# A three-layer sequence kernel on one core: slot outputs split over ScalarE and VectorE, the combine in fours, and the attention opening without its setup waits

## The chip, the cores and the metric

One core of one Trainium2 chip. The metric is the device time of one launch in microseconds (us), the median of several runs. Lower is better.

## What is computed

The reference, with names shortened, is a chain of four blocks over 4096 tokens of 256 features, each added to its input and followed by a layer norm. The inputs are float32.

```
x = _layernorm(x + conv_mlp(x))         # gated convolution block, then a two-layer MLP, 4 x 1024 tokens
x = _layernorm(x + experts(x))          # 32 experts, top 6 of a token, only 48 tokens per expert are served
x = _layernorm(x + attention(x))        # per branch of 1024 tokens: 16 heads of 16, rotary embedding
x = _layernorm(x + sparse_ffn(x))       # silu(gate) * up, 2 of each 4 kept, down

# in experts:
pos = jnp.take_along_axis(jnp.cumsum(oh, axis=0) - 1, flat_e[:, None], axis=1)[:, 0]
valid = pos < C                          # C = 48
slot = jnp.where(valid, flat_e * C + pos, E * C)
...
out = jnp.einsum('tk,tkh->th', topk_w.astype(x.dtype), y_pairs)
```

An expert serves the first 48 tokens that choose it, in token order. A token behind the point where all experts are full gets nothing from them. The chip's work on the expert outputs therefore touches only the first tiles of 128 tokens.

## The kernel before

The tokens are 32 tiles of 128 (`NT`), held in `x_sb` as [128, 32, 256]. Three functions follow one another: `conv_mlp_phase`, `experts_phase` and `attention_ffn_phase`. Each is a block in which every engine has its own program; the programs meet at semaphores only, and at a barrier between two blocks.

**End of the experts.** `experts_phase` computes 32 x 48 = 1536 slots. The experts' outputs lie transposed in `yT` (in the memory called arena). Twelve steps `j` (`CJ`) turn them: TensorE makes two 128x128 transposes into a PSUM bank `tp[j % 2]` (line 1038), VectorE multiplies them by the slots' weights into the high part `y[0]` (line 933, written in the matmul's float32r type), and VectorE again forms the low part `y[1]`, the product minus its high part (line 935). TensorE may fill the bank of step j once `y_ok` says that step j-2 is through with it. ScalarE's last instruction of the phase is the copy of the last expert's output (line 772).

**The combine.** A second block adds the slot outputs to the tokens. The generator `busy_pairs` (lines 1047 to 1056) is a loop over four groups of eight tiles with a branch on whether the group is reached by any slot, and in it a loop over four pairs of tiles with the same branch. In a pair, VectorE builds two one-hot matrices `hot[0]`, `hot[1]` of [128, 12, 128] (line 1068), TensorE sums 12 steps of high and low part for each tile into a bank of its own (line 1084, 24 matmuls per tile), and VectorE adds each bank to its tile (line 1074). A pair's one-hots wait until the pair before is summed (`cb_mm`), and its matmuls until the pair before is added (`cb_ok`). TensorE and VectorE load the branch's value from SBUF each for itself.

**Opening of the attention stage.** In `attention_ffn_phase` SyncE first starts the loads `mask`, `cos`, `sin`, `w_qk`, `w_v` (semaphore `consts`) and then four of the later weights. VectorE normalises the first branch's eight tiles in two halves (statistics at lines 1489 and 1495, the scaling at line 1504), with GpSimd computing the inverse deviation between (lines 1307 and 1310). GpSimd then fills constant columns of `v` and `qks` (lines 1323 to 1326; `setup` reaches 3 after them). VectorE casts the identity (line 1674) and writes eight constant columns (line 1678, `ready`). Both TensorE and ScalarE wait for `setup` 3 and `ready` 1 at their start:

```
            pe.wait_ge(consts, 16 * 5)
            pe.wait_ge(setup, 3)
            pe.wait_ge(ready, 1)
```

Then comes a loop over the eight tiles of the branch. TensorE transposes the tokens of a tile (line 1766, `x_transposed`, which waits for its half's layer norm through `ln_ok`), ScalarE copies them (line 1341), TensorE makes q, k and v (lines 1775 and 1777), ScalarE copies these (lines 1349 and 1352), VectorE rotates q and k (`rotate`, lines 1517 to 1524), ScalarE writes the high parts (line 1359 and two copies) and VectorE the low parts (`low_parts`, lines 1530 and 1531). VectorE's program has `rotate(0, t)` and `low_parts(0, t)` of one tile after another, so the rotation of the next tile follows the low parts of this one. When all eight are there, TensorE transposes q and k (`first_rows`, line 1782), finds the row maxima and starts the heads.

## Time and profile before

| | |
|---|---|
| median of 3 runs | 1910.19 us (1908.25 to 1912.74) |
| the profiled execution | 1904.56 us |
| its span, first to last instruction | 1902.7 us |
| mean granted clock of TensorE in it | 0.922 |
| busy: TensorE matmul / VectorE / ScalarE / GpSimd | 86% / 60% / 42% / 12% of the span |

The span is of one execution, and 1.9 us of its time lie around it. Times in the trace count from the start of the span. Busy shares are of the whole span, and a pipelined engine that is busy need not be at its best rate. PEclk is the share of TensorE's full clock of 2.4 GHz that the chip granted: 1.00 is 2.4 GHz, 0.50 is 1.2 GHz. What an engine waited for is inferred from the semaphores.

### The profile page before, as it was taken

How to read it: one execution, taken by the hardware profiler on the slowest of the kernel's cores; microseconds unless marked ns; L12 is line 12 of the kernel's file. 1: busy time of each engine (PE TensorE's matmuls, PEld its weight loads, DVE VectorE, ACT ScalarE, POOL GpSimd, SP SyncE). 2: the span in 40 equal slices, each digit the busy share in tenths (PEclk: the TensorE clock that was granted, in tenths of full speed). 3: DMA queues.
4: the chain of work that ended last, by engine and by line, in shares of the span. 5: the costliest groups of instructions: out<-in, count | busy, mean ns of one | idle time of the engine just before them, and what ended most of it. 6: DMA issues, size and time to landing. Idle time of an engine off the chain costs nothing.

```text
span 1902.7 us, 26419 instructions
## 1 busy us (share of the span) xinstructions
PE 1636.9 (86%) x10042; PEld 1007.7 (53%) x10043; DVE 1141.5 (60%) x2367; ACT 792.5 (42%) x1296; POOL 235.7 (12%) x237
## 2 busy tenths in 40 slices
PE   3899999986999964788899989899989899889797
PEld 3788888874558853333355433355433455433345
DVE  5556665647421144668558677568667578677465
ACT  5444444421212200437744157643167552177530
POOL 4333333311420001000000000100000100000100
PEclk8999999987999976759999989899989899988999
DMA  2000000005115502000000000000000000000000
GB/s 102 12 23 23 22 22 22 22 12 177 26 33 151 149 12 91 1 1 2 1 1 1 0 1 2 23 1 1 1 1 2 23 1 1 0 1 1 23 1 22
DMA packets 27147, 47.96 MB, mean 25 GB/s; under 512 B 7312, under 2 KB 16016, under 8 KB 26256
## 3 DMA queue, kind: packets, MB, share of 16 engines
q1 hardware_dynamic: 26464, 44.74, 7.4%
q0 software_dynamic: 576, 1.77, 0.3%
q8 instruction: 70, 1.15, 0.3%
q14 instruction: 37, 0.30, 0.0%
HBM read 37.59 MB, written 9.06 MB: 25 GB/s over the span
## 4 chain that ended last, share of the span: by engine, by line
issue 59%; POOL 2%; DVE 0%; POOLq 0%; DVEq 0%
POOL rs_sb L1310 1%; POOL ve_sb L1307 0%; POOL qks_sb L1325 0%; POOL v_sb L1324 0%; POOL qks_sb L1315 0%; DVE bn_sb L1489 0%; DVE x_sb_sb L1504 0%; POOLq L1144 0%; POOLq L65 0%; POOL qks_sb L1326 0%; DVE mv_sb L1495 0%; DVEq L1144 0%; POOL v_sb L1323 0%; DVEq L65 0%; DVEq L1493 0%
## 5 line engine op out<-in xcount | busy, mean ns | idle before, releaser
L1546 DVE TENSOR_REDUCE mx_sb<-s_ps 128x1 f32<-128x512 f32 (+1 forms) x512 | 313.0, 652 | 140.9 <-PE s_ps L1818 80.0
L1378 ACT ACTIVATE room_sb<-s_ps 128x1024 f32<-128x1024 f32 (+1 forms) x320 | 280.9, 950 | 21.6 <-PE s_ps L1842 20.5
L1815 PE MATMUL s_ps<-room_sb 48*128 48x512 f16 (+3 forms) x640 | 175.9, 345 | 25.1 <-DVE mx_sb L1546 16.8
L1862 PE MATMUL cm_ps<-room_sb,v_sb 128*32 128x512 f32 (+3 forms) x1536 | 167.4, 526 | 0.8 <-ACT room_sb L1384 0.8
L1842 PE MATMUL s_ps<-room_sb 51*128 51x128 f16 (+4 forms) x1152 | 123.5, 287 | 41.8 <-ACT room_sb L1378 34.9
L1307 POOL TENSOR_TENSOR ve_sb<-mv_sb,eps_sb 128x4 f32<-128x4 f32 x24 | 5.0, 210 | 1120.8 <-DVE mv_sb L1495 1120.8
L1985 PE MATMUL cm_ps<-w_fd_sb,room_sb 128*128 128x256 f32 x512 | 126.5, 394 | 14.7 <-DVE room_sb L1625 14.7
L1842 PEld LDWEIGHTS s_ps<-room_sb 50*128 50x128 f16 (+1 forms) x1152 | 39.1, 96 | 180.8 <-ACT room_sb L1378 145.0
L1815 PEld LDWEIGHTS s_ps<-room_sb 48*128 48x128 f16 x640 | 54.5, 97 | 145.8 <-DVE mx_sb L1546 97.1
L1972 PE MATMUL s_ps<-xbT_sb,w_fg_sb 128*128 128x512 f32 x256 | 128.9, 615 | 0.8 <-ACT xbT_sb L1415 0.8
L1972 PE MATMUL s_ps<-xbT_sb,w_fu_sb 128*128 128x512 f32 x256 | 127.1, 607 | 0.0
L392 DVE SCALAR_TENSOR_TENSOR x_sb_sb<-xp_sb,conv_w_sb,x_sb_sb 128x512 f32<-128x512 f32 x96 | 108.5, 1138 | 22.8 <-ACT x_sb_sb L319 20.5
L1985 PEld LDWEIGHTS cm_ps<-w_fd_sb,room_sb 128*128 128x128 f32 x512 | 93.9, 191 | 37.9 <-DVE room_sb L1625 14.0
L398 DVE SCALAR_TENSOR_TENSOR m1T_sb<-mm_ps,m1T_sb 128x512 fp32r<-128x512 f32 x64 | 44.3, 692 | 97.3 <-ACT m1T_sb L311 97.3
L953 PE MATMUL em_ps<-xT_sb,ws_gu_sb 128*128 128x512 f32 x192 | 90.3, 615 | 8.0 <-DMA rows<-zeros 8.0
L1420 ACT ACTIVATE sgl_sb<-s_ps 128x512 f32<-128x512 f32 x64 | 38.2, 597 | 134.7 <-PE s_ps L1972 134.6
L1818 PE MATMUL s_ps<-room_sb 51*128 51x128 f16 x512 | 80.6, 233 | 9.6 <-ACT room_sb L1368 9.2
L1541 DVE TENSOR_REDUCE mx_sb<-s_ps 128x2 f32<-128x512 f32 (+1 forms) x128 | 66.3, 555 | 23.6 <-PE s_ps L1818 23.6
L479 PE MATMUL mm_ps<-h1T_sb,w_up_sb 128*128 128x512 f32 x128 | 57.8, 452 | 22.9 <-DVE h1T_sb L416 22.9
L311 ACT ACTIVATE m1T_sb<-mm_ps 128x512 fp32r<-128x512 f32 x64 | 38.1, 595 | 80.7 <-PE mm_ps L481 80.7
L479 PE MATMUL ro_ps<-w_dn_sb,m1T_sb 128*128 128x256 f32 x256 | 71.5, 279 | 0.0
L480 PE MATMUL ro_ps<-w_dn_sb,m1T_sb 128*128 128x256 f32 x256 | 71.5, 279 | 0.0
(242 smaller groups left out, 3250.1 us busy)
## 6 DMA issues: line engine op xcount, KB each, us to landing
we_gu_sb<-we_gu SPq DMA_DIRECT2D x32, 352.0 KB
we_dn_sb<-we_dn SPq DMA_DIRECT2D x32, 176.0 KB
x_in_sb<-x SPq DMA_DIRECT2D x9, 512.0 KB, 3.6
rows<-x_sb_sb SPq DMA_DIRECT2D x8, 512.0 KB, 3.0
x_sb_sb<-rows SPq DMA_DIRECT2D x2, 2048.0 KB, 11.5
out<-x_sb_sb SPq DMA_DIRECT2D x8, 512.0 KB, 2.6
xp_sb<-w_in SPq DMA_DIRECT2D x1, 1024.0 KB, 5.5
x_sb_sb<-w_up SPq DMA_DIRECT2D x1, 1024.0 KB, 6.6
```

Source lines behind the costliest of these rows:

```text
L392: dve.scalar_tensor_tensor(xc[:, c, :], xp[:, c, k:k + GTOK], conv_w[:, c, k:k + 1], xc[:, c, :], ALU.mult, ALU.add)\
L479: pe.matmul(out, of[0][at], by[0][cols], start=start, stop=False)
L480: pe.matmul(out, of[1][at], by[0][cols], start=False, stop=False)
L953: last = pe.matmul(mm[c % 4][:, :], ws_gu[:, k, col:col + P], xT[:, k, g * GTOK:(g + 1) * GTOK], start=(k == 0), stop=(k == KD - 1))
L1378: act.activation(weights[(g * NU + u) % SLOTS_P][:, 2 * pair:2 * pair + 2, 0:width(u) * P], W[s % 2][:, :, 0:width(u) * P], ACT.Exp, scale ...
L1546: dve.tensor_reduce(mx[:, pair, k % 2, slot:slot + 1], X[:, k % 2, 0:count * P], AX.X, ALU.max, negate=True).then_inc(mx_ok, 1)
L1815: last = pe.matmul(X[:, k % 2, at * P:(at + plain) * P], query[head:head + NORM, i * P:(i + 1) * P], key[head:head + NORM, j * P:(j + plai ...
L1818: last = pe.matmul(X[:, k % 2, (at + plain) * P:(at + count) * P], query[head:head + USED, i * P:(i + 1) * P], key[head:head + USED, i * P ...
L1842: last = pe.matmul(W[s % 2][:, head, (at + low - i) * P:(at + high - i) * P], key[first:first + rows, j * P:(j + 1) * P], query[first:firs ...
L1862: last = pe.matmul(O[32 * h:32 * h + 32, (i - half * GT) * P:(i - half * GT + count) * P], v[:, j, g * HG + h, :], weights[(g * NU + u) % ...
L1972: last = pe.matmul(bank[:, e, :], wt[:, k, ch * P:(ch + 1) * P], xbT[:, k, g * 512:(g + 1) * 512], start=(k == 0), stop=(k == KD - 1))
L1985: last = pe.matmul(CM[:, t // 2, (t % 2) * D:(t % 2 + 1) * D], hs[:, k % 3 * 4 + i, t * P:(t + 1) * P], w_fd[:, k % 2 * 4 + i, :], start=( ...
```

## The change

1. `y[0]` is written by ScalarE (a scaled copy), `y[1]` still by VectorE. The transposes go to the four banks `mm[j % 4]` in place of two banks `tp[j % 2]`, and TensorE waits for step j-4.
2. The combine takes four tiles at a time (`QUAD`): `busy_quads`, four one-hot matrices, and four banks `total`, two of them the former `ro`, two from `mm`. The inner loop has two turns in place of four.
3. ScalarE's waits for `setup` and `ready` are gone. TensorE's stand behind the loop over the tiles. VectorE's wait for `setup` ahead of the cast is gone.

```diff
 GATHER_AT = 4
 SLOTS_AT = 5
 MOE_AT = 6
+QUAD = 4
 MOE_SLOTS = 2 * (GT + 2 * NSX) + GT
 TAKEN = 3.0e38
 
@@ -795,6 +796,10 @@
                     act.wait_ge(sub_ok, 1)
                     act.activation(ex, ex, ACT.Exp).then_inc(exp_ok, 1)
             expert_out(E - 1)
+            act.wait_ge(ws_ok, 2)
+            for j in range(CJ):
+                act.wait_ge(ty_ok, j + 1)
+                act.activation(y[0][:, j, :], mm[j % 4][:, 0:D], ACT.Copy, scale=w_slot[:, j:j + 1]).then_inc(ws_ok, 1)
 
         @block.vector
         def _(dve):
@@ -929,10 +934,8 @@
                     slot_weights()
             dve.wait_ge(ws_ok, 2)
             for j in range(CJ):
-                dve.wait_ge(ty_ok, j + 1)
-                dve.tensor_scalar(y[0][:, j, :], tp[j % 2][:, 0:D], w_slot[:, j:j + 1], None, ALU.mult).then_inc(ws_ok, 1)
                 dve.wait_ge(ws_ok, j + 3)
-                dve.scalar_tensor_tensor(y[1][:, j, :], tp[j % 2][:, 0:D], w_slot[:, j:j + 1], y[0][:, j, :],
+                dve.scalar_tensor_tensor(y[1][:, j, :], mm[j % 4][:, 0:D], w_slot[:, j:j + 1], y[0][:, j, :],
                                          ALU.mult, ALU.subtract).then_inc(y_ok, 1)
 
         @block.tensor
@@ -1032,10 +1035,10 @@
             expert_down(E - 1)
             pe.wait_ge(ey_ok, E)
             for j in range(CJ):
-                if j >= 2:
-                    pe.wait_ge(y_ok, j - 1)
+                if j >= 4:
+                    pe.wait_ge(y_ok, j - 3)
                 for k in range(KD):
-                    last = pe.transpose(tp[j % 2][:, k * P:(k + 1) * P],
+                    last = pe.transpose(mm[j % 4][:, k * P:(k + 1) * P],
                                         yT[:, k, j * CG:(j + 1) * CG, :].rearrange("p c e -> p (c e)"), ident[:])
                 last.then_inc(ty_ok, 1)
 
@@ -1044,16 +1047,17 @@
 
 
 
-        hot = [sb(f"hot{i}", [P, CJ, P], F32R) for i in range(2)]
-
-        def busy_pairs(eng):
+        hot = [sb(f"hot{i}", [P, CJ, P], F32R) for i in range(QUAD)]
+        total = [bank[:, 0, :] for bank in ro] + [bank[:, 0:D] for bank in mm[0:QUAD - 2]]
+
+        def busy_quads(eng):
 
             with eng.Fori(0, NT // 8) as o:
                 with eng.If(eng.value_load(busy[0:1, bass.ds(o * 8, 1)], min_val=0, max_val=P) > 0):
-                    with eng.Fori(0, 4) as m:
-                        r = o * 4 + m
-                        with eng.If(eng.value_load(busy[0:1, bass.ds(r * 2, 1)], min_val=0, max_val=P) > 0):
-                            yield Step(r, 2, 0)
+                    with eng.Fori(0, 8 // QUAD) as m:
+                        r = o * (8 // QUAD) + m
+                        with eng.If(eng.value_load(busy[0:1, bass.ds(r * QUAD, 1)], min_val=0, max_val=P) > 0):
+                            yield Step(r, QUAD, 0)
 
         block = ctx.enter_context(nc.Block())
 
@@ -1062,26 +1066,26 @@
             dve.tensor_tensor(rel[:, :, :], cnt[:, :].unsqueeze(1).to_broadcast([P, NT, CJ]),
                               base[:, :].unsqueeze(2).to_broadcast([P, NT, CJ]), ALU.subtract).then_inc(rel_ok, 1)
             dve.wait_ge(rel_ok, 1)
-            for r in busy_pairs(dve):
-                for i in range(2):
+            for r in busy_quads(dve):
+                for i in range(QUAD):
                     dve.wait_ge(cb_mm, r(1))
                     dve.tensor_tensor(hot[i][:, :, :], rel[:, bass.ds(r(1, i), 1), :].rearrange("p a j -> p (a j)")
                                       .unsqueeze(2).to_broadcast([P, CJ, P]),
                                       lane[:, :].unsqueeze(1).to_broadcast([P, CJ, P]), ALU.is_equal).then_inc(oh_ok, 1)
-                for i in range(2):
+                for i in range(QUAD):
                     dve.wait_ge(cb_mm, r(1, i + 1))
                     xt = x_sb[:, bass.ds(r(1, i), 1), :].rearrange("p a b -> p (a b)")
-                    dve.tensor_tensor(xt, ro[i][:, 0, :], xt, ALU.add).then_inc(cb_ok, 1)
+                    dve.tensor_tensor(xt, total[i], xt, ALU.add).then_inc(cb_ok, 1)
 
         @block.tensor
         def _(pe):
-            for r in busy_pairs(pe):
-                for i in range(2):
+            for r in busy_quads(pe):
+                for i in range(QUAD):
                     pe.wait_ge(oh_ok, r(1, i + 1))
                     pe.wait_ge(cb_ok, r(1))
                     for j in range(CJ):
                         for half in range(2):
-                            last = pe.matmul(ro[i][:, 0, :], hot[i][:, j, :], y[half][:, j, :],
+                            last = pe.matmul(total[i], hot[i][:, j, :], y[half][:, j, :],
                                              start=(j == half == 0), stop=(j == CJ - 1 and half == 1))
                     last.then_inc(cb_mm, 1)
 
@@ -1427,8 +1431,6 @@
 
             act.sem_inc(exp_ok, LEAD)
             act.sem_inc(ev_ok, LEAD)
-            act.wait_ge(setup, 3)
-            act.wait_ge(ready, 1)
             xt_copied(0, 0)
             for t in range(ST):
                 if t + 1 < ST:
@@ -1670,7 +1672,6 @@
             for s in range(2):
                 layernorm("x", 0, s)
             dve.wait_ge(consts, 16 * 5)
-            dve.wait_ge(setup, 3)
             dve.tensor_copy(ident_h[:, :], ident[:, :])
             by_group = qks[:, :, :, FILTER].rearrange("p t (g s h) -> p t g s h", g=NHG, s=2)
             for g in range(NHG):
@@ -1751,8 +1752,6 @@
             pe.sem_inc(pv_mm, LEAD)
             pe.sem_inc(bt_mm, LEAD)
             pe.wait_ge(consts, 16 * 5)
-            pe.wait_ge(setup, 3)
-            pe.wait_ge(ready, 1)
 
             def x_transposed(c, t):
                 k = c * ST + t
@@ -1997,6 +1996,8 @@
                 if t + 1 < ST:
                     x_transposed(0, t + 1)
                 qkv(0, t)
+            pe.wait_ge(setup, 3)
+            pe.wait_ge(ready, 1)
             for pair in range(2):
                 first_rows(0, pair)
             for_maxima(0, 0, 0, NX + 4)
```

The instructions in a row, as they are written for each engine, with the semaphores that they wait for (em is the `mm` of the experts, et its `tp`, er its `ro`; slot_weight_ready is `ws_ok`, out_transposed `ty_ok`, slot_out_ready `y_ok`).

VectorE at the end of the experts, before:

```order
L933 TENSOR_SCALAR y_sb<-et_ps,w_slot_sb 128x256 [waits out_transposed,slot_weight_ready]
L935 SCALAR_TENSOR_TENSOR y_sb<-et_ps,w_slot_sb,y_sb 128x256 [waits slot_weight_ready]
L933 TENSOR_SCALAR y_sb<-et_ps,w_slot_sb 128x256 [waits out_transposed]
L935 SCALAR_TENSOR_TENSOR y_sb<-et_ps,w_slot_sb,y_sb 128x256 [waits slot_weight_ready]
L1042 UNCONDITIONAL_BRANCH
```

The two middle kinds of row go on alternating, twelve of each. After the change VectorE has:

```order
L893 TENSOR_TENSOR su_sb<-em_ps,sg_sb 128x512 [waits shared_gu_done,shared_gate_ready]
L911 TENSOR_TENSOR ea_sb<-eg_sb,et_ps 88x96 [waits expert_down_done,expert_gate_ready] x7
L938 SCALAR_TENSOR_TENSOR y_sb<-em_ps,w_slot_sb,y_sb 128x256 [waits slot_weight_ready] x12
L1045 UNCONDITIONAL_BRANCH
L1064 UNCONDITIONAL_BRANCH [waits barrier_Pool_Activation_PE_DVE_SP_release]
L1066 TENSOR_TENSOR rel_sb<-cnt_sb,base_sb 128x384
```

and ScalarE, up to its first instructions of the attention stage:

```order
L768 ACTIVATE eg_sb<-et_ps 88x96 [waits expert_act_ready,expert_gu_done]
L773 ACTIVATE arena_sb<-et_ps 128x96 [waits expert_down_done] x2
L802 ACTIVATE y_sb<-em_ps,w_slot_sb 128x256 [waits out_transposed,slot_weight_ready]
L802 ACTIVATE y_sb<-em_ps,w_slot_sb 128x256 [waits out_transposed] x11
L1045 UNCONDITIONAL_BRANCH
L1339 UNCONDITIONAL_BRANCH [waits barrier_Pool_Activation_PE_DVE_SP_release]
L1345 ACTIVATE xt_sb<-s_ps 128x256 [waits x_transposed] x2
```

Twelve instructions left VectorE and stand on ScalarE, each VectorE instruction now waits for one of ScalarE's, and the first two copies of token transposes (line 1345 after, 1341 before) wait for the transposes alone.

TensorE in the combine loop and at the opening of the attention stage, before:

```order
L1055 COMPARE_AND_BRANCH
L1080 REGISTER_ALU
L1084 MATMUL er_ps<-y_sb,hot_sb 128x256 [waits combined,onehot_ready]
L1084 MATMUL er_ps<-y_sb,hot_sb 128x256 x23
L1080 REGISTER_ALU
L1084 MATMUL er_ps<-y_sb,hot_sb 128x256 [waits combined,onehot_ready]
L1084 MATMUL er_ps<-y_sb,hot_sb 128x256 x23
L1055 UNCONDITIONAL_BRANCH
...
L1749 UNCONDITIONAL_BRANCH [waits barrier_Pool_Activation_PE_DVE_SP_release]
L1766 MATMUL s_ps<-ident_sb,x_sb_sb 128x128 [waits rows_set_up3,layernorm_done,setup3,consts3]
L1766 MATMUL s_ps<-ident_sb,x_sb_sb 128x128
```

and after:

```order
L1088 MATMUL er_ps<-y_sb,hot_sb 128x256 [waits combined,onehot_ready]
L1088 MATMUL er_ps<-y_sb,hot_sb 128x256 x23
L1084 REGISTER_ALU
L1088 MATMUL em_ps<-y_sb,hot_sb 128x256 [waits combined,onehot_ready]
L1088 MATMUL em_ps<-y_sb,hot_sb 128x256 x23
L1084 REGISTER_ALU
L1088 MATMUL em_ps<-y_sb,hot_sb 128x256 [waits combined,onehot_ready]
L1088 MATMUL em_ps<-y_sb,hot_sb 128x256 x23
L1059 UNCONDITIONAL_BRANCH
...
L1750 UNCONDITIONAL_BRANCH [waits barrier_Pool_Activation_PE_DVE_SP_release]
L1765 MATMUL s_ps<-ident_sb,x_sb_sb 128x128 [waits layernorm_done,consts3]
L1765 MATMUL s_ps<-ident_sb,x_sb_sb 128x128
```

The body of the loop has four times 24 matmuls in place of two times 24 (the first 24 are above the rows shown). Behind the loop the first transpose waits for the layer norm and the constants only; rows_set_up3 (`ready`) and setup3 moved to the first transposes of q and k.

## Rows read from the trace of the kernel before

**Rows 1.** The page, busy time of each engine (share of the span, instructions).

```profile
PE 1636.9 (86%) x10042; PEld 1007.7 (53%) x10043; DVE 1141.5 (60%) x2367; ACT 792.5 (42%) x1296; POOL 235.7 (12%) x237
```

**Rows 2.** Slot outputs: lines 933, 935 (ns min/median/max, first and last start), timeline.

```profile
L933 DVE TENSOR_SCALAR y_sb<-et_ps,w_slot_sb x12: 474/474/484, 677.5 to 687.6; 128x256 fp32r<-128x256 f32 x12
...
L935 DVE SCALAR_TENSOR_TENSOR y_sb<-et_ps,w_slot_sb,y_sb x12: 483/484/485, 678.0 to 688.1; 128x256 fp32r<-128x256 f32 x12
...
676.74 1.10 PE L1038 MATMUL et_ps<-ident_sb,arena_sb 128*128 128x128 f32 x4 [0.42 <-ACT arena_sb L772]
```

**Rows 3.** ScalarE groups by form: count, busy us, mean ns, idle before.

```profile
L317 ACT ACTIVATE xp_sb<-mm_ps 128x512 f32<-128x512 f32 x31 | 18.5, 597 | 0.0
...
L319 ACT ACTIVATE x_sb_sb<-mm_ps,conv_b_sb,conv_w_sb 128x512 f32<-128x512 f32 x31 | 24.4, 788 | 0.0
...
L1352 ACT ACTIVATE v_sb<-s_ps 128x256 f32<-128x256 f32 x8 | 3.0, 379 | 0.0
```

**Rows 4.** Timeline of the combine: start us, us, engine, line, [idle before <- releaser].

```profile
691.84 3.43 DVE L1068 TENSOR_TENSOR hot_sb<-rel_sb,lane_sb 128x1536 fp32r<-128x1536 f32 x2 [2.41 <-issue]
...
698.52 0.42 DVE L1074 TENSOR_TENSOR x_sb_sb<-er_ps,x_sb_sb 128x256 f32 x1 [3.26 <-PE er_ps L1084]
...
701.40 0.42 DVE L1074 TENSOR_TENSOR x_sb_sb<-er_ps,x_sb_sb 128x256 f32 x1 [2.45 <-PE er_ps L1084]
...
704.61 7.27 PE L1084 MATMUL er_ps<-y_sb,hot_sb 128*128 128x256 f32 x48 [3.36 <-DVE hot_sb L1068]
```

**Rows 5.** Windows, one per pair of tiles: us, busy of each engine, PEclk.

```profile
688.87:702.80 13.93, 7.59 (x48) 7.39 (x48) 4.84 (x6) 0.00 (x0) 0.00 (x0) 0.70 0.00 0
702.80:713.42 10.62, 7.27 (x48) 7.07 (x48) 4.27 (x4) 0.00 (x0) 0.00 (x0) 0.84 0.00 0
713.42:725.37 11.95, 8.60 (x48) 8.40 (x48) 4.28 (x4) 0.00 (x0) 0.00 (x0) 0.71 0.00 0
725.37:739.01 13.64, 7.50 (x48) 7.30 (x48) 4.28 (x4) 0.00 (x0) 0.00 (x0) 0.85 0.00 0
```

**Rows 6.** Opening of the attention stage: timeline, and one line of the DMA issues.

```profile
740.80 0.43 SPq L1294 DMA_DIRECT2D w_v_sb<-w_v  x1
...
743.36 1.38 DVE L1504 TENSOR_SCALAR x_sb_sb<-x_sb_sb,mv_sb,rs_sb 128x256 f32<-128x256 f32 x4 [1.68 <-POOL rs_sb L1310]
...
748.09 6.20 DVE L1504 TENSOR_SCALAR x_sb_sb<-x_sb_sb,mv_sb,rs_sb 128x256 f32<-128x256 f32 x4 [1.49 <-POOL rs_sb L1310]
...
749.79 2.87 POOL L1325 MEMSET qks_sb<- 128x3328 f16 x1
...
754.35 0.82 DVE L1678 CAST qks_sb<-mask_sb 128x32 f16<-128x32 f32 x8
...
755.43 0.66 PE L1766 MATMUL s_ps<-ident_sb,x_sb_sb 128*128 128x128 f32 x2 [20.74 <-DVE qks_sb L1678]
...
763.39 0.69 DVE L1517 TENSOR_TENSOR ro_sb<-qk_sb,cos_sb 128x512 f32<-128x512 f32 x1 [8.22 <-ACT v_sb L1352]
...
w_v_sb<-w_v SPq DMA_DIRECT2D x1, 256.0 KB, 4.4
```

**Rows 7.** Timeline of the loop over the first branch's tiles.

```profile
765.02 0.38 PE L1766 MATMUL s_ps<-ident_sb,x_sb_sb 128*128 128x128 f32 x2
...
767.53 0.69 DVE L1517 TENSOR_TENSOR ro_sb<-qk_sb,cos_sb 128x512 f32<-128x512 f32 x1
...
767.82 0.38 PE L1766 MATMUL s_ps<-ident_sb,x_sb_sb 128*128 128x128 f32 x2
...
789.61 0.69 DVE L1517 TENSOR_TENSOR ro_sb<-qk_sb,cos_sb 128x512 f32<-128x512 f32 x1
```

**Rows 8.** Windows of the first branch's heads, before and after the clock rises.

```profile
835.50:847.40 11.90, 10.56 (x73) 3.72 (x74) 5.52 (x9) 5.75 (x7) 0.00 (x0) 0.50 0.01 1
847.40:949.00 101.60, 89.80 (x926) 35.57 (x927) 72.15 (x156) 81.08 (x96) 1.55 (x4) 1.00 0.01 1
```

**Rows 9.** TensorE's waits from 115 to 350 us: in total, times, longest.

```profile
PE mm_ps L479 <- DVE h1T_sb L416: 15.1, 5, 3.0
```

## The prediction

> **What bounds the kernel now.** I read the page first. TensorE is busy 86% of the span and VectorE 60% [rows 1], but a share of the whole span says nothing of three short stretches, so the rest comes from the timeline of 676 to 794 us. All work passes through them one behind the other: experts, barrier, combine, barrier, attention. A microsecond saved there is saved at the end, unless a later wait takes it back.
>
> Slot outputs, 676.7 to 688.6 us. VectorE's two instructions of a step take 0.47 and 0.48 us. Their twelve starts run from 677.5 to 687.6 and from 678.0 to 688.1, so a step is 10.1 / 11 = 0.92 us, and VectorE is full. TensorE's four first transposes together take 1.10 us, 0.55 per step [rows 2]; after them it waits for VectorE.
>
> Combine, from 691.84 us on. A pair is a chain: a one-hot matrix, 48 matmuls, one addition, the turn of the loop. TensorE stands still 3.36 us from one pair's last matmul to the next pair's first [rows 4]. It is busy 7.59, 7.27, 8.60 and 7.50 us in the four pairs, at a mean clock of 0.70 to 0.85 [rows 5]. That is half clock first and full clock later: the second tile of the first pair ends 701.40 - 698.52 = 2.88 us behind the first [rows 4], so the first tile took 7.59 - 2.88 = 4.7 us.
>
> Opening of attention, 739 to 794 us. The tokens' first half is normalised at 743.36 + 1.38 = 744.74 us, yet the first transpose starts at 755.43, right behind the constant columns that end at 754.35 + 0.82 = 755.17. The rotation of the first tile then waits 8.22 us more, until 763.39 [rows 6]. From there the loop is no longer TensorE's: its tile takes 767.82 - 765.02 = 2.80 us, while the rotations stand (789.61 - 767.53) / 6 = 3.68 us apart, and the first one 767.53 - 763.39 = 4.14 us [rows 7].
>
> **Slot outputs.** Removed: twelve times 0.47 us on VectorE. Added: twelve scaled copies on ScalarE. No such copy of 128x256 is in the trace. Below it lies the plain copy, 0.38 us. Above it: 128x512 costs 0.60 us plain and 0.79 us with scale and bias from SBUF [rows 3], so at most 0.38 + 0.19 = 0.57 us; I take 0.47, half of the surcharge, as one operand of the two is used. ScalarE has nothing behind these but the barrier. A bank's round is now transposes (0.55 to 0.7 us), copy 0.47, low part 0.48 and three hand-overs that I put at 0.1 each (the opening's first, 755.17 to 755.43, is 0.26 [rows 6]), near 1.9 us; over four banks that is 0.47 us per step. TensorE's own 0.55 is more and sets the step. From 676.74 the last low part then ends after 12 x 0.55 + 0.1 + 0.47 + 0.1 + 0.48 = 7.75 us, at 684.5, in place of 688.6: **4.1 us**. If the clock stays high and the step is 0.47 us, it is 5.0. If copies take 0.57 us and each hand-over is fully exposed on one engine (0.7 us a step), 2.3.
>
> **Combine.** The additions, one-hots and 192 matmuls are the same; the first two groups of four are the eight tiles that four pairs cover now. Two turns with their idle go: 2 x 3.36 = 6.7 us. Two starts at half clock go too. A quad is a pair (mean of 7.59, 7.27, 8.60 and 7.50: 7.74 us) and two more tiles at full clock, 7.74 + 2 x 2.88 = 13.5 us. Twice that is 27.0 against 30.96 us: 4.0. Together **10.7 us**. VectorE hides four one-hots at no cost as long as TensorE is slower: two take 3.43 us, so the fourth is ready 7 us after the first starts, and TensorE wants it 1.8 + 4.7 + 2 x 2.88 = 12.3 us after. If that cover went, 1.7 us per tile would show. The range is 6.7 (every later tile at half clock's price) to 12.5 (second quad entered with the clock still high).
>
> **Opening.** TensorE's queue now starts with the first half's layer norm, 744.74, and the constants; of these `w_v` is issued at 740.80 and lands 4.4 us later [rows 6], 745.2. From first transpose to first rotation took 763.39 - 755.43 = 7.96 us, so q, k and v of tile 0 are there at 753.2. VectorE is not there before 755.2: its program still has the second half's scaling (6.20 us for four instructions, while GpSimd fills the constant columns) and the columns themselves [rows 6]. So 2.0 of the 10.2 us by which TensorE starts earlier are covered, and what is late next is VectorE. The rotation moves from 763.39 to 755.2: 8.2 us. With copies of the second tile done in time the first spacing is 3.68 as the others, 0.5 more. **8.7 us**. The moved waits are long past at `first_rows` and cost nothing; without the wait on `setup` VectorE gains nothing, since its scaling ends last. Bounds: 6.7 if VectorE were 2.0 us later with its scaling, 10.7 if it were through by 753.2.
>
> The sum is 4.1 + 10.7 + 8.7 = 23.5 us. Against the profiled execution, 1904.56, that is 1881.1. The median of the runs shown is 5.6 us higher, 1910.19, so I forecast **1886.7 us**. A difference of about 0.2% (3.8 us) is what a measurement of this kernel can tell from none.
>
> **The rivals.**
>
> *The opening runs at half clock.* TensorE would work on tiles with short pauses between. Before, it reached full clock at its second tile and held it through gaps of the 3.68 us cadence. If it stayed at 1.2 GHz, a tile would take 5.6 us, more than VectorE's 3.68, and the loop would end at 745.2 + 1.3 + 8 x 5.6 + 4 = 795.3, in place of 789.61 + 3.6 = 793.2 [rows 7]. The term of 8.7 turns into -2.1: 1897.5 us. For it: the start has idle TensorE before it. Against: so had the start before. The Trainium skill, "TensorE: Matmul & The Clock Gate", section "A second HAM failure mode: psum-queue depth-cycling", says that short idles between groups of matmuls can make the clock swing. By that rule this case would be the likely one; the rows of the old loop speak against it. 8%.
>
> *A longer loop body costs time at its turn.* The combine's body doubles on TensorE, and a turn might wait for instructions. In the convolution's loop, whose body is over ten times as long, no wait of TensorE from 115 to 350 us is above 3.0 us, and all name VectorE [rows 9]. One turn left, one entry and one exit at up to 3.0 us each beyond the cover: at most 9, likelier 3, so 1889.7. The Trainium skill, "Runtime: NRT & Kernel Launch", section "Instruction fetch mechanics", has this rule: a taken branch whose target isn't in the pages held must fetch it. 5%.
>
> *The clock rises late in the heads.* This is the case on the other side. In the first branch the clock is low until 847.4 us. Just before, ScalarE is busy 5.75 of 11.9 us; behind, 81.08 of 101.6 [rows 8]. At half clock the heads thus run at 0.48 / 0.80 = 0.6 of their pace, and a microsecond of them costs 0.65 more. If the rise didn't come in this branch, that would be 101.6 x 0.65 = 66 us, 1886.7 + 66 = 1953. It decides once the low stretch takes in 23.5 / 0.65 = 36 us of work more. For it: all of the stage moves by 23 us. Against: TensorE is busy 10.56 of 11.9 us just ahead of the rise, and nothing of that work is changed. 2%. The same mechanism the other way, the rise one unit of work (11.9 us) earlier, gives back 11.9 x 0.4 = 5, and 1881.9: 10%.
>
> *The change does only part of what it says*: the quads run, but the slot outputs keep their step, as each step still passes TensorE, ScalarE and VectorE one after another. 1890.8 us, 5%.
>
> **How the numbers follow.** The forecast with its three terms has 70%. The low ends of the terms (2.3, 6.7, 6.7) give 1894.5 and the high ends (5.0, 12.5, 10.7) 1882.0; the runs before spread 2 to 3 us around their median. With the earlier rise the low end is near 1877. The half-clock opening lies at 1897.5, and I let the range stop a little short of it: 1877 to 1896. Only the late clock, and a few mishaps together, are not faster by 3.8 us: faster 0.95, same 0.03, slower 0.02.
>
> **What would show it.** The transposes of line 1041 and the low parts of line 938 come every 0.5 to 0.6 us, and the low parts end within 8 us. Two turns of the combine instead of four, 2 x (1.8 + 13.5 + 0.4) + 1 = 32 to 33 us from first one-hot to last addition, with TensorE at 1.00 in the last three tiles of each. The first transpose of tokens some 6 us after the stage starts in place of 16, and the first rotation right behind the constant columns, waiting for nothing. Rotations stay 3.68 us apart. Wrong: a rotation that waits for ScalarE at the start, spacing above 4 us, PEclk 0.50 there, a turn above 4 us, or a low-clock stretch of the heads that differs by over 5 us.

## The result, and the profile of the kernel after

| | before | after |
|---|---|---|
| median of 5 runs each on the same chip, us | 1908.47 (1898.01 to 1912.74) | 1878.90 (1875.38 to 1887.31) |
| ratio, 95% interval | | 0.9853 [0.9826, 0.9880] |
| profiled execution, us | 1904.56 | 1887.31 |
| its span, us | 1902.7 | 1885.2 |

The change makes the kernel 1.47% faster: 28 us by the ratio (23 to 33), 29.6 us by the medians. The profiled execution of after is the slowest of its five runs, so its span is only 17.5 us shorter; where the missing part went is told below. The page answers to [rows 1]: VectorE has 12 instructions less and ScalarE 12 more.

```profile
PE 1636.9 (87%) x10042; PEld 1007.5 (53%) x10043; DVE 1134.7 (60%) x2355; ACT 798.1 (42%) x1308; POOL 236.0 (13%) x237
```

In each trace I measured four stretches between five fixed events: first transpose of the slot outputs, first block-start instruction of VectorE behind the barrier (`rel`), first statistics of attention, first rotation, first transpose of `first_rows`. All in us:

| | slot outputs | barrier and combine | statistics to rotation | rotations to `first_rows` | sum |
|---|---|---|---|---|---|
| before | 12.14 | 50.46 | 24.06 | 29.87 | 116.53 |
| after | 6.76 | 38.74 | 15.60 | 29.63 | 90.73 |
| gained | 5.4 | 11.7 | 8.5 | 0.2 | 25.8 |

**Slot outputs.** Two lines by source (ns min/median/max, starts), then the timeline. They answer to [rows 2].

```profile
L802 ACT ACTIVATE y_sb<-em_ps,w_slot_sb x12: 468/476/478, 683.5 to 688.2; 128x256 fp32r<-128x256 f32 x12
```
```profile
L938 DVE SCALAR_TENSOR_TENSOR y_sb<-em_ps,w_slot_sb,y_sb x12: 473/474/484, 684.1 to 688.7; 128x256 fp32r<-128x256 f32 x12
```
```profile
682.76 5.37 PE L1041 MATMUL em_ps<-ident_sb,arena_sb 128*128 128x128 f32 x24 [0.42 <-ACT arena_sb L773]
...
684.14 5.07 DVE L938 SCALAR_TENSOR_TENSOR y_sb<-em_ps,w_slot_sb,y_sb 128x256 fp32r<-128x256 f32 x12 [3.02 <-ACT y_sb L802]
...
685.40 3.24 ACT L802 ACTIVATE y_sb<-em_ps,w_slot_sb 128x256 fp32r<-128x256 f32 x8 [0.16 <-PE em_ps L1041]
```

The timeline joins instructions that follow without a gap. VectorE's twelve low parts are one row of 5.07 us: from its first one on, VectorE waits for nothing, and it takes one every 0.42 us. TensorE's 24 transposes are one row of 5.37 us, 0.45 us per step. The last low part ends 684.14 + 5.07 - 682.76 = 6.45 us behind the first transpose; it was 11.9 us.

**Combine.** The timeline answers to [rows 4], the windows (columns: us; busy of PE, PEld, DVE, ACT, POOL; PEclk, DMA share, GB/s) to [rows 5].

```profile
692.50 6.76 DVE L1072 TENSOR_TENSOR hot_sb<-rel_sb,lane_sb 128x1536 fp32r<-128x1536 f32 x4 [2.41 <-issue]
...
694.31 8.43 PE L1088 MATMUL er_ps<-y_sb,hot_sb 128*128 128x256 f32 x48 [6.18 <-DVE hot_sb L1072]
...
710.03 6.76 DVE L1072 TENSOR_TENSOR hot_sb<-rel_sb,lane_sb 128x1536 fp32r<-128x1536 f32 x4 [0.97 <-issue]
...
711.84 6.02 PE L1088 MATMUL er_ps<-y_sb,hot_sb 128*128 128x256 f32 x48 [3.35 <-DVE hot_sb L1072]
...
723.77 0.42 DVE L1078 TENSOR_TENSOR x_sb_sb<-em_ps,x_sb_sb 128x256 f32 x1 [2.45 <-PE em_ps L1088]
```
```profile
694.31:699.50 5.19, 5.19 (x24) 5.19 (x25) 4.95 (x3) 0.00 (x0) 0.00 (x0) 0.50 0.00 0
...
711.84:717.70 5.86, 5.86 (x48) 5.86 (x49) 5.29 (x4) 0.00 (x0) 0.00 (x0) 1.00 0.00 0
```

One turn with TensorE idle is left, 3.35 us. The first four tiles start at PEclk 0.50 and take 14.2 us (694.31 to 702.58 + 5.92). The second four start at 1.00 and take 11.8 us. From first one-hot to the end of the last addition it is 723.77 + 0.42 - 692.50 = 31.69 us, in place of 43.41.

**Opening of attention.** Timeline, answering to [rows 6, 7].

```profile
728.26 1.41 DVE L1491 BATCH_NORM_STATS2 bn_sb<-x_sb_sb 128x6 f32<-128x256 f32 x4 [4.07 <-PEq L606]
...
733.77 0.69 PE L1765 MATMUL s_ps<-ident_sb,x_sb_sb 128*128 128x128 f32 x2 [10.15 <-DMA w_v_sb<-w_v]
...
736.62 6.32 DVE L1506 TENSOR_SCALAR x_sb_sb<-x_sb_sb,mv_sb,rs_sb 128x256 f32<-128x256 f32 x4 [1.49 <-POOL rs_sb L1314]
736.62 1.75 POOL L1328 MEMSET v_sb<- 128x1920 f32 x1
...
738.32 2.87 POOL L1329 MEMSET qks_sb<- 128x3328 f16 x1
...
739.70 0.38 ACT L1356 ACTIVATE v_sb<-s_ps 128x256 f32<-128x256 f32 x1
...
742.99 0.83 DVE L1679 CAST qks_sb<-mask_sb 128x32 f16<-128x32 f32 x8
...
743.86 0.69 DVE L1519 TENSOR_TENSOR ro_sb<-qk_sb,cos_sb 128x512 f32<-128x512 f32 x1
...
747.53 0.69 DVE L1519 TENSOR_TENSOR ro_sb<-qk_sb,cos_sb 128x512 f32<-128x512 f32 x1
```

The first transpose of tokens starts 5.5 us behind the first statistics, released by the transfer of `w_v`; it was 16.1. ScalarE has copied q, k and v of the first tile at 739.70 + 0.38 = 740.08. VectorE is not there: it scales until 742.94, casts the columns, and rotates at 743.86 without a wait. The second rotation follows 3.67 us later. One source line shows what held VectorE (ns min/median/max), and two windows how the clock went on in the loop:

```profile
L1506 DVE TENSOR_SCALAR x_sb_sb<-x_sb_sb,mv_sb,rs_sb x96: 394/407/5202, 731.9 to 1881.8; 128x256 f32<-128x256 f32 x96
```
```profile
747.60:751.00 3.40, 3.37 (x6) 1.83 (x7) 2.67 (x6) 2.00 (x6) 0.00 (x0) 0.50 0.00 0
751.00:768.10 17.10, 12.82 (x43) 6.92 (x41) 13.38 (x29) 10.03 (x27) 0.00 (x0) 1.00 0.00 0
```

One of the scalings takes 5202 ns where the median is 407. TensorE works on the first tile at 0.50 and is at 1.00 from 738 us on. The clock falls once more in the loop, for 3.4 us, right where TensorE goes on with q, k and v of its fourth tile after 2.87 us of waiting, and comes back; the rotations keep their 3.67 to 3.68 us.

**The rest of the span.** The three terms give 25.8 us, the spans differ by 17.5. Ahead of the slot outputs the profiled run of after is 6.0 us later (682.76 against 676.74), in code that is the same. One window of before and the same one of after show where most of it arises:

```profile
600.00:640.00 40.00, 38.46 (x325) 33.23 (x324) 4.39 (x14) 9.54 (x29) 2.35 (x1) 1.00 0.52 157
```
```profile
600.00:640.00 40.00, 38.46 (x264) 32.59 (x263) 3.20 (x11) 7.61 (x23) 2.35 (x1) 0.81 0.46 136
```

The clock of this window is 1.00 in the one and 0.81 in the other, and TensorE, busy 38.46 of 40 us in both, gets 264 matmuls done in place of 325. Further on, the heads' exponentials to the output projection take 122.6 in place of 120.3 us. 6.0 - 25.8 + 2.3 = -17.5. The low-clock stretch of the first branch moved along and hardly changed its length (58.0 us before, 54.6 after):

```profile
789.40:847.40 58.00, 42.77 (x237) 17.03 (x238) 37.50 (x70) 16.16 (x19) 0.00 (x0) 0.50 0.00 1
```
```profile
768.10:822.70 54.60, 37.91 (x202) 15.13 (x203) 35.55 (x67) 15.33 (x19) 0.00 (x0) 0.50 0.00 1
```

### The profile page after: what moved, and what is told of

It reads as the page before. It is cut to its first block, busy times and chain, and to the rows that moved or that the text cites. A ratio compares the mean times of both kernels' runs of the same rounds, so it can differ in the third digit from the quotient of the medians.

```text
span 1885.2 us, 26388 instructions
## 1 busy us (share of the span) xinstructions
PE 1636.9 (87%) x10042; PEld 1007.5 (53%) x10043; DVE 1134.7 (60%) x2355; ACT 798.1 (42%) x1308; POOL 236.0 (13%) x237
## 3 DMA queue, kind: packets, MB, share of 16 engines
q0 software_dynamic: 576, 1.77, 0.3%
## 4 chain that ended last, share of the span: by engine, by line
issue 59%; POOL 2%; DVE 0%; POOLq 0%; DVEq 0%
POOL rs_sb L1314 1%; POOL ve_sb L1311 0%; POOL qks_sb L1329 0%; POOL v_sb L1328 0%; DVE bn_sb L1491 0%; POOL qks_sb L1319 0%; DVE x_sb_sb L1506 0%; POOLq L1148 0%; POOLq L65 0%; POOL qks_sb L1330 0%; DVE mv_sb L1497 0%; DVEq L1148 0%; POOL v_sb L1327 0%; DVEq L65 0%; DVEq L1495 0%
## 5 line engine op out<-in xcount | busy, mean ns | idle before, releaser
L1984 PE MATMUL cm_ps<-w_fd_sb,room_sb 128*128 128x256 f32 x512 | 130.7, 403 | 14.6 <-DVE room_sb L1627 14.6
```

The costliest lines, as they stand in the source:

```text
L1984: last = pe.matmul(CM[:, t // 2, (t % 2) * D:(t % 2 + 1) * D], hs[:, k % 3 * 4 + i, t * P:(t + 1) * P], w_fd[:, k % 2 * 4 + i, :], start=( ...
```

## The experiments

Times and ratios stand beside runs of the kernel before on the same chip: 1906.22 us for the first four, 1907.17 for the next four, 1905.11 for the last four. The four columns of the table above, for each trace, in us:

| | slot outputs | combine | to rotation | to `first_rows` | sum |
|---|---|---|---|---|---|
| x1_slots | 6.77 | 51.57 | 22.36 | 29.87 | 110.57 |
| x2_quads | 12.10 | 39.78 | 22.43 | 29.87 | 104.18 |
| x3_opening | 12.10 | 50.52 | 15.62 | 29.66 | 107.90 |
| x4_four_banks | 12.09 | 50.56 | 24.02 | 29.87 | 116.54 |
| x5_two_banks | 11.47 | 50.93 | 23.77 | 29.98 | 116.15 |
| x6_columns_late | 6.76 | 38.73 | 13.61 | 30.12 | 89.22 |
| x7_eights | 6.77 | 32.90 | 15.33 | 29.65 | 84.65 |
| x8_no_turn | 6.77 | 46.45 | 15.79 | 29.65 | 98.66 |
| x9_eights_late | 6.94 | 33.43 | 13.49 | 30.13 | 83.99 |
| x10_warm | 6.77 | 32.92 | 12.66 | 30.12 | 82.47 |
| x11_setup_wait | 6.73 | 38.78 | 15.57 | 29.64 | 90.72 |
| x12_change_again | 7.00 | 39.64 | 15.49 | 29.67 | 91.80 |

### Each part of the change alone

The kernel before with one part of the change's diff: x1 has the scaled copies on ScalarE and four banks, x2 the quads, x3 the moved waits of attention.

> The kernel before with the first part of the change alone (ScalarE writes the high parts, four banks). Theory: the three parts are links of one chain and add up; this one gives what it gave in the profile of the change: transposes to the block behind them 6.8 us in place of 12.1, so 5.4 us off the time. Rival A, the parts need each other (TensorE that leaves this stretch earlier only meets a lower clock in the combine): the combine behind it is longer by as much, and the time within 1 us of before. Rival B, most of the measured gain of the whole change is clock luck in stages it doesn't touch: this stretch shows 5.4 us less and the time varies by 5 us either way.

> The kernel before with the second part alone (the combine by four tiles). Theory: 11.7 us less from the first one-hot to the last addition (31.7 in place of 43.4), of it 6.7 for two turns, 4.0 for the two starts at half clock that go, and about 1.8 because the second four start at full clock; time 10 to 12 us down. Rival: the second four starting at full clock was chance; then the gain is 10 us and the first tile of the second four takes 4.5 us or more.

> The kernel before with the third part alone (waits of the opening). Theory: from the stage's first statistics to the first rotation 15.6 us in place of 24.1, rotations 3.7 us apart, 8.5 to 8.7 us off the time. Rival: TensorE reaches full clock later when its start is moved ahead and the loop over tiles gives back 2 us or more.

Measured: 1898.20 us, ratio 0.9966 [0.9952, 0.9981]; 1894.56, 0.9935 [0.9910, 0.9959]; 1896.83, 0.9940 [0.9916, 0.9963]. As shares of 1906 us that is 6.5, 12.4 and 11.4 us, together 30.3 beside 28.1 for the whole. The parts add up within their intervals. In the table each part moves its own column by 5.4, 10.7 and 8.4 us; in the whole these columns move by 5.4, 11.7 and 8.5.

Three entries move without an edit. In x1 the combine is 1.1 us longer, by the clock: the matmuls of its four pairs take 32.1 us, before 31.0. In x1 and x2 the opening is 1.7 and 1.6 us shorter: the clock rises while TensorE makes q, k and v of the first tile (its `v` matmuls take 1.03 us, 1.78 before), and in x1 the scaling beside GpSimd's fills ends earlier (5.85 us, 6.20 before). In x2, besides, the clock does not stay high in the second quad as it did in after:

```profile
711.01 7.52 PE L1086 MATMUL er_ps<-y_sb,hot_sb 128*128 128x256 f32 x48 [3.34 <-DVE hot_sb L1070]
```
```profile
711.00:715.00 4.00, 3.99 (x21) 3.99 (x22) 4.00 (x3) 0.00 (x0) 0.00 (x0) 0.58 0.00 0
```

7.52 us in place of 6.02, after an idle of 3.34 us beside 3.35. So x2's combine takes 32.38 us, after's 31.69. The term has a part of about 1 us that comes and goes with the clock. Within the quads it is more: in after the first quad started slower than in x2 (14.2 us beside 13.4) and the second faster (11.8 beside 13.3).

### Slot outputs: four banks without ScalarE, ScalarE without four banks

x4, against the kernel before; VectorE keeps both instructions, and both read `mm[j % 4]`:

```diff
-                dve.tensor_scalar(y[0][:, j, :], tp[j % 2][:, 0:D], w_slot[:, j:j + 1], None, ALU.mult).then_inc(ws_ok, 1)
+                dve.tensor_scalar(y[0][:, j, :], mm[j % 4][:, 0:D], w_slot[:, j:j + 1], None, ALU.mult).then_inc(ws_ok, 1)
...
-                if j >= 2:
-                    pe.wait_ge(y_ok, j - 1)
+                if j >= 4:
+                    pe.wait_ge(y_ok, j - 3)
```

x5, against the kernel before; the banks stay `tp[0]` and `tp[1]`:

```diff
+                act.activation(y[0][:, j, :], tp[j % 2][:, 0:D], ACT.Copy, scale=w_slot[:, j:j + 1]).then_inc(ws_ok, 1)
...
-                dve.tensor_scalar(y[0][:, j, :], tp[j % 2][:, 0:D], w_slot[:, j:j + 1], None, ALU.mult).then_inc(ws_ok, 1)
```

> The kernel before with four banks for the slot outputs but both instructions still on VectorE. Theory: VectorE is full there, so a step stays 0.91 to 0.92 us and nothing is gained (12.1 us from first transpose to the next block, less than 0.5 us off). Rival: the gain is the deeper buffering, which hides the hand-over between TensorE and VectorE; then the step falls towards 0.55 us and most of the 5.4 us comes with VectorE doing both.

> The kernel before with ScalarE writing the high parts but the two banks of before. Theory: a step is a round of a bank (transposes 0.69, copy 0.4, low part 0.48, three hand-overs near 0.1: 1.9 us) over the number of banks, so 0.9 us with two and the stretch to the next block stays 11.5 to 12.3 us; both halves of the first part are needed. Rival: moving the instruction alone frees VectorE and gives most of the 5.4 us (stretch below 9 us).

Measured: x4 1909.03 us, one run, stretch 12.09. x5 1910.45 us, one run, stretch 11.47. The timelines of the two:

```profile
681.77 0.48 DVE L933 TENSOR_SCALAR y_sb<-em_ps,w_slot_sb 128x256 fp32r<-128x256 f32 x1
...
682.68 0.47 DVE L933 TENSOR_SCALAR y_sb<-em_ps,w_slot_sb 128x256 fp32r<-128x256 f32 x1
```
```profile
680.76 1.11 PE L1040 MATMUL et_ps<-ident_sb,arena_sb 128*128 128x128 f32 x4 [0.80 <-DVE y_sb L937]
681.48 0.90 ACT L801 ACTIVATE y_sb<-et_ps,w_slot_sb 128x256 fp32r<-128x256 f32 x2 [1.01 <-PE et_ps L1040]
681.99 0.91 DVE L937 SCALAR_TENSOR_TENSOR y_sb<-et_ps,w_slot_sb,y_sb 128x256 fp32r<-128x256 f32 x2 [0.90 <-ACT y_sb L801]
...
682.53 1.11 PE L1040 MATMUL et_ps<-ident_sb,arena_sb 128*128 128x128 f32 x4 [0.66 <-DVE y_sb L937]
```

In x4 VectorE runs without a gap, 682.68 - 681.77 = 0.91 us per step, as before: banks alone give nothing. In x5 no engine is full. TensorE fills both banks, then waits 0.66 to 0.80 us for the low part of a bank, and so on in rounds of 682.53 - 680.76 = 1.77 us for two steps, 0.885 per step. Both halves are needed: ScalarE takes work off VectorE, and the other two banks let three engines work on different steps.

### Combine: one loop body of eight tiles

Against the kernel after: no inner loop; VectorE builds four one-hots, then adds tile i and builds the one-hot of tile i + 4; the last wait is TensorE's.

```diff
+                    yield Step(o, OCT, 0)
...
-                    dve.tensor_tensor(xt, total[i], xt, ALU.add).then_inc(cb_ok, 1)
+                    dve.tensor_tensor(xt, total[i % QUAD], xt, ALU.add).then_inc(cb_ok, 1)
+                    if i + QUAD < OCT:
+                        one_hot(i + QUAD)
...
-                    pe.wait_ge(cb_ok, r(1))
+                    pe.wait_ge(cb_ok, r(1, max(i - QUAD + 1, 0)))
```

> The changed kernel with eight tiles per turn of the combine (one loop, four banks and four one-hot matrices used in turn). Theory: the remaining idle of TensorE between the fours, 3.35 us, goes, and one value load with its branch (about 0.9 us) at the entry and at each of the three groups not reached is no more than before: first one-hot to last addition 28.3 us in place of 31.7, time 3 to 5 us below the changed kernel. Rival: eight tiles of one-hots on VectorE between the additions make VectorE the bound (a tile 0.42 + 1.75 + hand-overs above 2.88 us), then 31 us or more.

Measured: 1868.49 us, ratio 0.9809 [0.9792, 0.9826]; first one-hot to last addition 27.03 us in place of 31.69. The timeline:

```profile
685.35 6.76 DVE L1069 TENSOR_TENSOR hot_sb<-rel_sb,lane_sb 128x1536 fp32r<-128x1536 f32 x4 [1.35 <-issue]
...
694.37 5.92 PE L1091 MATMUL em_ps<-y_sb,hot_sb 128*128 128x256 f32 x48
...
697.57 0.42 DVE L1079 TENSOR_TENSOR x_sb_sb<-em_ps,x_sb_sb 128x256 f32 x1 [0.79 <-PE em_ps L1091]
697.91 1.75 DVE L1069 TENSOR_TENSOR hot_sb<-rel_sb,lane_sb 128x1536 fp32r<-128x1536 f32 x1
```

TensorE has no idle row behind its start, and goes at 2.88 us per tile; VectorE waits 0.79 us for it before an addition. A tile costs VectorE 0.42 + 1.75 = 2.2 us, so TensorE is the bound at full clock. The stretch is 4.7 us shorter. Of this 3.35 us are the idle of the turn that is gone; most of the other 1.3 us is the clock at the start, as the first two tiles take 687.16 to 694.37, 7.2 us, where after's took 694.31 to 702.58, 8.3 us. Beside x12, whose stretch is 32.59 us, it is 5.6 us. With one loop level less the entry is shorter too: VectorE stands 1.35 us before its first one-hot, not 2.41. The table has 6.1 us less than after in all (90.73 - 84.65). The ratios, 0.9809 beside 0.9853 and 0.9863, say 8 to 10 us, more than the 3 to 5 that were expected; what the rest is was not found out.

### Combine: what a pair's edge costs without the loop's turn

Against the kernel after: inside the body of four, the second pair waits for the first.

```diff
+                    if i == 2:
+                        for k in range(2):
+                            dve.wait_ge(cb_mm, r(1, k + 1))
...
-                    dve.wait_ge(cb_mm, r(1))
+                    dve.wait_ge(cb_mm, r(1, i // 2 * 2))
...
-                    pe.wait_ge(cb_ok, r(1))
+                    pe.wait_ge(cb_ok, r(1, i // 2 * 2))
```

> The changed kernel, with a loop body of four tiles but the waits of pairs inside it (the third one-hot waits until the first two tiles are summed and added). Theory: what costs is the chain over one-hot, matmuls and addition, not the turn: the gap of TensorE between the pairs inside the body is 3.36 - 0.97 = 2.4 us, and first one-hot to last addition 41.5 us against 43.4 with pairs and 31.7 with fours. Rival: the turn is the price, and most of the 11.7 us come back (below 35 us). A third possibility: a gap of 2.4 us is short enough for the clock to stay at 1.00, then 37.5 us.

Measured: 1882.51 us, one run; first one-hot to last addition 39.39 us.

```profile
700.19 6.02 PE L1093 MATMUL em_ps<-y_sb,hot_sb 128*128 128x256 f32 x48 [2.30 <-DVE hot_sb L1077]
...
709.56 8.62 PE L1093 MATMUL er_ps<-y_sb,hot_sb 128*128 128x256 f32 x48 [3.35 <-DVE hot_sb L1077]
...
720.46 6.02 PE L1093 MATMUL em_ps<-y_sb,hot_sb 128*128 128x256 f32 x48 [2.29 <-DVE hot_sb L1077]
```
```profile
700.19:708.70 8.51, 6.02 (x48) 5.81 (x48) 3.42 (x4) 0.00 (x0) 0.00 (x0) 1.00 0.01 2
708.70:715.50 6.80, 5.94 (x28) 5.95 (x29) 2.78 (x3) 0.00 (x0) 0.00 (x0) 0.50 0.00 0
```

This parts the 3.35 us: without the turn the idle is still 2.30 us (the last matmul, the addition, the next one-hot). The turn adds 1.05, of which 0.97 is VectorE's row "issue" at 710.03 in after. The 39.39 us lie between the 41.5 of the theory and the 37.5 of the third possibility, which came half true: the clock keeps 1.00 over the idle of 2.3 us (a pair takes 6.02 us), and is at 0.50 behind the one of 3.35 us (8.62 us). So quads save two waits of 3.35 us, and with them two occasions at which the clock can fall.

### Opening: the columns later, and the wait on `setup` put back

Both against the kernel after. x6, GpSimd fills the columns only behind both halves' layer norm:

```diff
+            pool.wait_ge(ln_ok, 2)
             pool.memset(v[:, :, :, HD:HD + 1], 1.0)
```

x11:

```diff
             dve.wait_ge(consts, 16 * 5)
+            dve.wait_ge(setup, 3)
             dve.tensor_copy(ident_h[:, :], ident[:, :])
```

> The changed kernel with GpSimd's fills of constant columns waiting until VectorE has scaled both halves. Theory: the 5.2 us instruction of VectorE's second scaling is stalled by these fills, so the four take 1.4 us as the first four do, and the first rotation comes when q, k and v of tile 0 are there, 12 us behind the first statistics in place of 15.6: 3 to 4 us off the time. Rival: the fills stall whatever VectorE does then, the first rotation or the constant columns, for the same 5 us, and nothing is gained.

> The changed kernel with VectorE's wait for the constant columns of GpSimd (setup) put back. Theory: VectorE's scaling ends behind the fills that stall it, so the wait is over when it is reached: first statistics to first rotation 15.6 us again, within 0.1. Rival: that wait was part of the gain, and 16 us or more are seen.

Measured: x6 1874.37 us, ratio 0.9843 [0.9825, 0.9861]; x11 1881.79 us, one run, statistics to rotation 15.57. The timeline of x6:

```profile
730.64 1.38 DVE L1507 TENSOR_SCALAR x_sb_sb<-x_sb_sb,mv_sb,rs_sb 128x256 f32<-128x256 f32 x4 [1.49 <-POOL rs_sb L1314]
...
732.07 0.83 DVE L1680 CAST qks_sb<-mask_sb 128x32 f16<-128x32 f32 x8
732.08 1.07 POOL L1328 MEMSET v_sb<- 128x128 f32 x1 [1.56 <-DVE x_sb_sb L1507]
...
734.70 2.86 POOL L1330 MEMSET qks_sb<- 128x3328 f16 x1
...
735.91 0.69 DVE L1520 TENSOR_TENSOR ro_sb<-qk_sb,cos_sb 128x512 f32<-128x512 f32 x1 [3.02 <-ACT v_sb L1357]
...
740.06 0.69 DVE L1520 TENSOR_TENSOR ro_sb<-qk_sb,cos_sb 128x512 f32<-128x512 f32 x1
```

The four scalings take 1.38 us instead of 6.32, with the same data and no fill of GpSimd beside them. In after, the three fills of 1.75, 2.87 and 0.55 us add up to 5.17 us, and the one scaling lasts 5.20: VectorE stands still for as long as GpSimd writes. In x1, x3 and x7 the same wait is split: the first three scalings overlap the three fills one by one and take 1.89 or 1.90, 3.03 and about 0.7 us, and all four take 5.85 us in x1. It works the other way too: the fill of 128x128 takes 1.07 us beside the casts, 0.32 alone. The rotations are not touched, 0.69 us beside the fill of 2.86. The Trainium skill, "SBUF — State Buffer", section "SBUF: two separate sides", has this as an exclusive lock on a port pair that VectorE's two-port modes and GpSimd share, where an instruction of VectorE with two inputs contends only if GpSimd reads. The traces agree, though no run shows which mode the scaling runs in: the one-input scalings wait, and the two-input rotations keep 0.69 us beside a fill that reads nothing. The page has the lock held for one instruction, as x1, x3 and x7 show it; one scaling that waits for three fills in a row, as in after, is more than it says.

The rotation comes 2.0 us earlier, not the 5 us that the scaling lost, since it now waits 3.02 us for ScalarE's copy: TensorE makes the first tile at half clock (0.50 from 728 to 734 us), and the second rotation follows only 4.15 us later. That gives 1.5 us in the sum, where 3 to 4 were expected. By its time x6 can't be told from the change (0.9843 beside 0.9853 and 0.9863). x11 leaves everything as it was: the wait on `setup` was free once the scaling ends behind it, so no part of the gain is due to its removal on VectorE.

### All together, the clock before the opening, and the change once more

x9 is x6 and x7 in one kernel. x12 is the kernel after, unchanged. x10 is x9 with 20 transposes of the identity, whose result nothing reads, before TensorE's wait for the constants:

```diff
+            for i in range(20):
+                pe.transpose(C[:, 0:P], ident[:], ident[:])
             pe.wait_ge(consts, 16 * 5)
```

> The changed kernel with both: eight tiles per turn, and the constant columns behind VectorE's scaling. Theory: links of one chain, so 6.1 + 1.5 us less: 83 us for the stretch that takes 90.7, and 6 to 9 us below the changed kernel in time. Rival: the clock takes it back, since TensorE's first tile of the opening then ends the wait and is slow when its clock is: 84.5 us or more, no less than with eight tiles alone.

> The kernel with both and, besides, twenty transposes of the identity into an unused bank at the start of TensorE's program of the attention stage, while it waits for the layer norm. Theory: q, k and v of tile 0 were late because TensorE made them at 1.2 GHz; busy before, it has PEclk 1.00 there or soon after, its first tile takes 3 to 4 us less, the first rotation comes 11 us behind the first statistics or sooner (13.6 with the columns late alone), and the stretch takes 80 to 81 us. Rival: the clock doesn't rise in time (six us of transposes aren't enough, or the few us of idle behind them let it fall); then 83 us or more, and the twenty transposes may themselves delay the first tile.

> The changed kernel itself, unaltered, on the chip of the next three. Theory: 24 to 30 us below before, and from the first transpose of the slot outputs to the first transposes of q and k 90.7 us again, within 2 us (what differs is when the clock rises in the opening). Rival: the profile shown of it was a lucky one, and its second four tiles start at half clock in another execution: then 92 to 93 us.

Measured: x9 1867.92 us, ratio 0.9782 [0.9748, 0.9816]; x10 1869.29, 0.9810 [0.9774, 0.9847]; x12 1882.20, 0.9863 [0.9830, 0.9895]. x9 beats both kernels: its interval lies below that of the change on the same chip. The medians are 14.3 us apart, and the stretch shows 91.80 - 83.99 = 7.8 us of it; the rest is not explained, and the six executions of x9 run from 1860.18 to 1884.89 us. x10 cannot be told from x9. Its windows:

```profile
716.00:720.50 4.50, 4.46 (x20) 4.06 (x20) 2.66 (x11) 0.00 (x0) 1.25 (x2) 0.50 0.53 156
720.50:724.00 3.50, 1.54 (x6) 0.87 (x7) 2.24 (x10) 0.77 (x2) 0.93 (x2) 0.99 1.04 350
724.00:727.40 3.40, 3.40 (x7) 1.92 (x6) 2.26 (x13) 0.00 (x0) 1.85 (x3) 0.50 1.01 417
727.40:733.00 5.60, 5.60 (x21) 3.38 (x20) 3.07 (x7) 3.42 (x9) 4.84 (x7) 1.00 0.44 181
```

The 4.5 us of transposes raise the clock, it is 0.99 when the first real work comes, and then it falls again for 3.4 us just when q, k and v of the first tile are made. The window ahead of that has TensorE busy for 1.54 of 3.5 us, waiting for `w_v` and for ScalarE's copies. The rotation came 0.8 us earlier; I had hoped for 3 to 4 us on the first tile. The sum is 1.5 us less, but 0.7 of that lies ahead of the added transposes.

## Why the prediction was right, and where it was not

The forecast was 1886.7 us with 1877 to 1896, the median is 1878.9, near the low end. Against the difference of 29.6 us my 23.5 is a fifth short. The three terms were right as mechanisms, and two of them were sized too small, by 1.3 and 1.0 us. Of the 7.8 us between forecast and median these are 2.3; 1.7 are the kernel before, 1908.47 and no longer 1910.19; the other 3.8 no term explains. All three terms at their high ends gave 1882.0. The range went on to 1877 for an earlier rise of the clock in the heads, which did not come. That the median, 3.1 us below 1882.0, still lies inside is in part luck.

- **Slot outputs, forecast 4.1, measured 5.4**, beyond the upper bound of 5.0. The step that failed is "TensorE's own 0.55 is more and sets the step". I divided the 1.10 us of the first four transposes by two; but the row holds the whole length of the last one, 0.42 us by its group's median (the 24 of line 1038). The pace is (1.10 - 0.42) / 3 = 0.23 us per transpose, 0.45 per step. And not TensorE set the step: VectorE's low parts follow one another at 0.42 us, closer than their length of 0.47, so their records overlap, and TensorE's weight loads wait for the banks that they hold. ScalarE's copy at 0.476 us was forecast as 0.47.
- **Combine, forecast 10.7 (6.7 to 12.5), measured 11.7.** The turns went as forecast, 2 x 3.36. The clock's part was put at 4.0 and is 5.0: I gave both quads a start at half clock and 13.5 us, and in this run the first took 14.2 and the second, without such a start, 11.8. The second was the upper case of the range. In x2 and x12, where it had one, the stretch takes 32.38 and 32.59 us, and the term is 10.8 to 11.0. The cover for the one-hots held: VectorE is late for nothing but the first. "32 to 33 us from first one-hot to last addition" held in x2 and x12; after, at 31.69, is just below.
- **Opening, forecast 8.7, measured 8.7**, of it 8.5 to the first rotation and 0.2 behind it. The steps are right: released by `w_v` 5.5 us behind the statistics (forecast 5.9), VectorE late next, first spacing 3.67. One size was off and cost nothing, as VectorE ends the wait: q, k and v are there 743.82 - 740.08 = 3.7 us before VectorE's columns end, not 2.0, since TensorE took 6.3 us from the first transpose to them, not 7.96, its clock being high from 738 us on. x6 shows that the scaling beside the fills was the reason, x11 that the wait on `setup` was not.
- **The half-clock opening did not come.** The clock did swing once in the loop (747.6 to 751.0, window above), and it cost nothing: VectorE sets the pace, and the rotations stayed 3.67 to 3.68 us apart over it. It fell behind a wait of 2.87 us that the loop of before did not have: VectorE was late, ScalarE waited 3.10 us for its first rotation, and TensorE for ScalarE's next copy of tokens. After it 17.1 us went at 1.00, with waits of at most 0.7 us. So the rival had a mechanism that exists, and a price that I took from a loop wholly at half clock, which did not occur. The section of the Trainium skill that the prediction names beside it, "TensorE: Matmul & The Clock Gate", "A second HAM failure mode: psum-queue depth-cycling", has the clock swing with short idles between groups of matmuls; the trace agrees in the one swing, and not for the waits of up to 0.7 us behind it.
- **The longer body costs nothing at its turn.** TensorE stands 3.35 us there, 3.36 before, though its body doubled. x7 doubles it again, but runs that body once, so it shows its entry alone, without a loss; a turn behind it was not measured.
- **The late clock in the heads did not come**, and not the early one either: 54.6 us at 0.50, 58.0 before. `first_rows` to first exponential is 42.2 us in both.
- **Only part of what it says** fell by x1: the slot outputs give their 5.4 us alone.

What the forecast had no term for is that executions of one kernel differ by more than a term. The three terms give 25.8 us in the traces, and the times 28 to 30. That is within the interval of 23 to 33, and the single executions of one kernel lie 6 to 25 us apart; between the two profiled ones, the clock in the experts' stage, which nobody edited, makes 6.0 us. The same kernel once more, x12, gave 22.9 us by the medians and 26 by the ratio, with an interval of 20 to 32. Whether something more than the three stretches was gained stays open: the runs don't resolve 3 us.

## What to carry to other kernels

Price a chain of stages in rotating buffers by the spacing of starts, not by the length of a group: a group's row holds one full latency that the next one overlaps. In a loop whose edge leaves TensorE idle, the edge costs its idle and, often, a slower clock behind it, so longer bodies, or one-hots kept a few tiles ahead of the matmuls, can gain twice. And look at what GpSimd writes while VectorE does one-input work: held back by under two microseconds, the same fills no longer stopped VectorE, though only 2.0 of the 5 us came through to the next step.

## What was not expected of the hardware

- A VectorE instruction of 0.41 us lasted 5.20 us beside fills of GpSimd (after), or the wait was shared out over four instructions, the longest of 3.03 us (x1, x3, x7). Two-input instructions beside the same fills kept their 0.69 us (x6).
- The clock stayed at 1.00 over TensorE's idles of 2.30 and 2.29 us in x8. Behind 3.35 us it was at 0.50 in x8, at 1.00 in after, and fell right behind the start in x2. The same four tiles thus take 11.8 us in after and 13.3 in x2.
- Raising the clock ahead of time did not hold it (x10): 4.5 us of transposes at 0.50, then 0.99, then 3.4 us at 0.50 again.
- The first branch runs 58.0 us at half clock before and 54.6 after, while, in the latter, VectorE is busy 35.55 us and TensorE 37.91. Whether that could be avoided wasn't tried.
